# A block of four gated layers on one core: the second layer's projection in fp32, small inputs as rows, and a new order of the work

## The reference

```python
x = x + tanh(g_xattn[0]) * wkv(w, u, k=_layernorm(x), v=ctx_2048)          # a scan over 64 steps per sequence
x = x + tanh(g_ffn[0])   * ffn(_layernorm(x), w_gate_up, w_proj)
x = x + tanh(g_xattn[1]) * attention(_layernorm(x), ctx_2048, mask)
x = x + tanh(g_ffn[1])   * linear_fp8(_layernorm(x), weight, weight_scale, bias)

def ffn(x, w_gate_up, w_proj):             # hidden width 1024
    gate, up = split(x @ ternary_quant(w_gate_up).T)
    h = silu(gate) * up
    hn = h * rsqrt(mean(h * h) + eps)      # eps of float32
    return hn @ ternary_quant(w_proj).T
```

## Time and profile before

| | |
|---|---|
| median of the runs | 175.01 us |
| the profiled execution: device time, span from its first to its last instruction | 174.68 us, 172.9 us |
| busy of the span: PE, DVE, ACT, POOL | 120.4, 135.1, 72.5, 54.4 us |
| granted clock of TensorE, mean | 0.868 |
| chain that ended last, by engine | DVE 56%, PE 20%, issue 8%, DMA 6%, ACT 4%, POOL 2% |

### The profile page before, as it was taken

How to read it: one execution, slowest core, us unless ns; L and a number is a source line. 1 busy time by engine, 2 the same in 40 slices (tenths; PEclk the granted TensorE clock), 3 DMA queues, 4 the chain that set the end, 5 groups by cost and what they waited for, 6 DMA issues and landing times.

```text
span 172.9 us, 2109 instructions
## 1 busy us (share of the span) xinstructions
PE 120.4 (70%) x723; PEld 80.6 (47%) x729; DVE 135.1 (78%) x275; ACT 72.5 (42%) x122; POOL 54.4 (31%) x69
## 2 busy tenths in 40 slices
PE   6549980961069397298960999796988596894672
PEld 6447750840055152045630656363666385681451
DVE  0485997799959859999999947999968868933950
ACT  2333555485034438033360455663951125514322
POOL 5085033006000004130493519635442303400320
PEclk9987997598555879969997599999999969999698
DMA  3599910000000000000000000000000000000033
GB/s 93 146 365 353 327 39 2 0 0 0 0 0 0 0 0 4 0 0 2 0 0 4 2 0 0 0 2 4 0 0 0 0 4 0 0 2 0 0 121 125
DMA packets 8045, 6.90 MB, mean 40 GB/s; under 512 B 2273, under 2 KB 7778, under 8 KB 8034
## 3 DMA queue, kind: packets, MB, share of 16 engines
q1 hardware_dynamic: 7602, 6.75, 12.4%
q10 hardware_dynamic: 432, 0.00, 0.1%
HBM read 5.71 MB, written 1.05 MB: 39 GB/s over the span
## 4 chain that ended last, share of the span: by engine, by line
DVE 56%; PE 20%; issue 8%; DMA 6%; ACT 4%; POOL 2%; SPq 2%; DVEq 1%; ACTq 0%
DVE sums L1005 6%; DVE sums L1097 6%; DMA xs<-in_x_dram 6%; DVE stats L978 5%; DVE xn L990 5%; DVE xs L1025 5%; DVE hbuf L1091 4%; DVE wsign L1067 4%; PE ps L759 3%; PE ps L758 3%; DVE wmask L1066 3%; PE ps L779 3%; DVE wmask L1072 2%; DVE ratio L1010 2%; DVE kv L1322 2%
## 5 line engine op out<-in xcount | busy, mean ns | idle before, releaser
L758 PE MATMUL ps<-xhi,wT 128*128 128x512 f16 x64 | 25.9, 404 | 7.8 <-DVE wT L1056 4.4
L759 PE MATMUL ps<-xlo,wT 128*128 128x512 f16 x64 | 26.2, 410 | 0.0
L779 PE MATMUL ps<-wT,wgu_raw 128*128 128x256 bf16 x64 | 16.6, 298 | 6.1 <-DVE wT L1056 4.3
L536 ACT ACTIVATE wgu_raw<-hbuf 128x512 f16<-128x512 f32 x16 | 10.0, 627 | 24.7 <-DVE hbuf L1091 24.6
L978 DVE BATCH_NORM_STATS2 stats<-xs 128x6 f32<-128x256 f32 x32 | 12.2, 409 | 6.6 <-DMA xs<-in_x_dram 6.4
L1091 DVE SCALAR_TENSOR_TENSOR hbuf<-ps,pscale,sil 128x512 f32<-128x512 f32 x16 | 12.0, 749 | 6.3 <-PE ps L759 3.5
L779 PE MATMUL ps<-wT,sums 128*128 128x256 bf16 x64 | 16.6, 297 | 0.0
L412 POOL TENSOR_TENSOR sqsum<-sqsum,ratio 128x512 f32<-128x512 f32 x8 | 11.4, 1429 | 15.5 <-ACT ratio L539 15.2
L1097 DVE TENSOR_TENSOR sums<-hbuf,wgu_raw 128x512 f16<-128x512 f32 x16 | 15.8, 989 | 0.0
L531 ACT ACTIVATE sil<-ps 128x512 f32<-128x512 f32 x16 | 9.5, 592 | 12.5 <-PE ps L759 12.0
L758 PEld LDWEIGHTS ps<-xhi,wT 128*128 128x128 bf16 x64 | 6.5, 102 | 16.8 <-DVE wT L1056 4.9
(11 more groups left out here) (151 smaller groups left out, 281.5 us busy)
## 6 DMA issues: line engine op xcount, KB each, us to landing
wgu_raw<-in_L_ffn_w_gate_up_dram SPq DMA_DIRECT2D x4, 512.0 KB, 8.9
xs<-in_x_dram SPq DMA_DIRECT2D x2, 512.0 KB, 8.0
ctx_sb<-in_ctx_dram SPq DMA_DIRECT2D x2, 512.0 KB, 8.8
wp_raw<-in_L_ffn_w_proj_dram SPq DMA_DIRECT2D x1, 1024.0 KB, 10.1
out_dram<-xs SPq DMA_DIRECT2D x4, 256.0 KB, 2.2
wlin_raw<-in_L_ffn_weight_dram SPq DMA_DIRECT2D x1, 256.0 KB, 9.3
bias_bc<-in_L_ffn_bias_dram SPq DMA_DIRECT2D x1, 128.0 KB, 8.9
mask_u<-in_mask_BxS_bk_dram SPq DMA_DIRECT2D x2, 32.0 KB, 7.9
```

The source lines that it names most:

```text
L536: act.activation(hhi[:, h, j, :], hbuf[:, b, :], ACT.Copy).then_inc(hhi_ready, 1)
L758: pe.matmul(ps[:, 4 + 2 * b + up, :], w, xhi[:, h, c, :], start=(c == 0), stop=False)
L759: mm = pe.matmul(ps[:, 4 + 2 * b + up, :], w, xlo[:, h, c, :], start=False, stop=(c == CH - 1))
L779: mm = pe.matmul(ps[:, i // 2, o:o + C], part[:, h, j, i * P:(i + 1) * P], wp, start=(first and j == 0 and i % 2 == 0), stop=(not first an ...
```

## The change

- **Projection in fp32.** `ffn_mul` writes the product in fp32 into `hidden` (two tiles, one for each half) and multiplies by silu alone. `hhi`, `hlo`, `hbuf`, `ffn_low` and the ACT copy are gone; so is `pscale` with all that computes it. ACT makes an fp32 copy `wpf` of the two quantized pairs of w_proj (`project_weight`), and `project(h, j)` is 4 fp32 matmuls of 256 columns. Squares are taken from `hidden`.
- **Small inputs as rows.** Decay, bonus, gates, weight scale, mask and bias are loaded as one row each by ACT's queue, behind a table load. PE spreads them by matmuls of one row (`spread_rows`, `spread_mask`); POOL converts the mask row, ACT makes `mask_add` of it. The decay's matmul takes one fp32 row in place of three bf16 ones. x half 0 comes in two transfers.
- **A new order.** DVE runs `wkv(2)` before `mix_out(0)`, quantizes whole pairs in the order 0, 1, 4, 2, 3, 5 with the clip in front, takes `xn_low(0)` before `wkv(3)`, and leaves the normalization of the ffn input wholly to ACT. PE starts the projections earlier, and sends `spread_greatest` before the last `residual_back` and the warming matmuls. 32 warming transposes become 16 and 4; one group of 8 warming matmuls is gone.

```diff
 def ffn_mul(n):
-    if n >= 2:
-        dve.wait_ge(sq_ready, n - 1)
-        dve.wait_ge(hlo_ready, n - 1)
-    dve.scalar_tensor_tensor(out=hbuf[:, b, :], in0=ps[:, 5 + 2 * b, :], scalar=pscale[:, 0:1],
-                             in1=sil[:, b, :], op0=ALU.mult, op1=ALU.mult).then_inc(h_ready, 1)
-def ffn_low(n):
-    dve.tensor_tensor(hlo[:, h, j, :], hbuf[:, b, :], hhi[:, h, j, :], ALU.subtract).then_inc(hlo_ready, 1)
+    dve.tensor_tensor(hidden[n // HT][:, n % HT, :], ps[:, 5 + 2 * b, :], sil[:, b, :],
+                      ALU.mult).then_inc(h_ready, 1)
...
+def project_weight(a):          # ACT
+    act.wait_ge(wq_ready, QUANT_ORDER.index(GU_PAIRS + a) + 1)
+    act.activation(wpf[:, a, :], wT[:, GU_PAIRS + a, :], ACT.Copy).then_inc(wpf_ready, 1)
...
 def project(h, j):              # PE
-    pe.wait_ge(hlo_ready, h * HT + j + 1)
+    pe.wait_ge(wpf_ready, 1 + j // 4)
+    pe.wait_ge(h_ready, h * HT + j + 1)
     for i in range(TPC):
-        for part, first in ((hhi, True), (hlo, False)):
-            mm = pe.matmul(ps[:, i // 2, o:o + C], part[:, h, j, i * P:(i + 1) * P], wp, ...)
+        mm = pe.matmul(ps[:, i // 2, o:o + C], hidden[h][:, j, i * P:(i + 1) * P], wp, ...)
...
+def spread_rows():              # PE
+    pe.wait_ge(in_rows, 80)
+    for c in range(CH):
+        pe.matmul(wcol[:, c:c + 1], w_row[0:1, c * P:(c + 1) * P], ones_row[0:1, 0:1], ...)
+        pe.matmul(ucol[:, c:c + 1], u_row[0:1, c * P:(c + 1) * P], ones_row[0:1, 0:1], ...)
+    pe.matmul(ps[:, 1, 4:9], ones_row[0:1, :], g_row[0:1, 0:5], ...).then_inc(cols_ps, 1)
...
 # DVE's order from the second layer's quantization on
-weights_clip(4); weights_clip(5); gate_up_bound()
-wkv(3); quant_sign(0); quant_sign(1); xn_low(0); power_of_two()
+quant(0); quant(1); xn_low(0); wkv(3)
+dve.tensor_reduce(valid[:, :], mask_add[:, :, :], AX_X, ALU.max)
+quant(2)
...
 # PE's order
+gate_up(2); project(0, 0); gate_up(3); project(0, 1); y_back(1); project(0, 2)
+gate_up(4); project(0, 3); gate_up(5); gate_up(6)
 pe.wait_ge(res_ready[1], 2)
 channel_major(1, 2, TPC, TPC, 2, xnT_ps)
 project(0, 4)
+gate_up(7)
 project(0, 5); project(0, 6); gate_up(HT)
+project(0, 7)
 gate_up(HT + 1)
-project(0, 7)
...
 residual_back(2)
+spread_greatest()
 residual_back(3)
-pe.wait_ge(xn3T_ready, 2 * CH)
-keep_warm(WARM_LAST, 4, wT)
-spread_greatest()
+keep_warm(WARM_LAST, 5, wT)
```

More of the change, by code:

```diff
@@ L163, in gated_blocks @@
         res = xs
-        in_x = [sem("in_x0"), sem("in_x1")]
+        in_x = [sem(f"in_x{i}") for i in range(3)]
         in_ctx = [sem("in_ctx0"), sem("in_ctx1")]
@@ L273, in gated_blocks @@
         wlin_t = w_lin.rearrange("(o p) i -> p o i", p=P)
-        mask_t = mask.rearrange("(i two) m -> two i m", two=2)
+        mask_t = mask.rearrange("(a i two) m -> a i two m", a=1, two=2)
         ROW_GROUPS = [0, 2, 1, 3]
-        def act_scales(p):
-            return p + 1 if p == 0 else p
+        QUANT_ORDER = (0, 1, 4, 2, 3, 5)
         LAST_ORDER = (0, 1, 3, 2)
@@ L591, in _ @@
             softmax_exp(0)
+            square(CHUNKS * HT - 1)
             attn_in(0)
@@ L620, in _, with spread_mask @@
         def _(pe):
+            def spread_rows():
+                pe.wait_ge(const_ready, 1)
+                pe.wait_ge(in_rows, 80)
+                for c in range(CH):
+                    pe.matmul(wcol[:, c:c + 1], w_row[0:1, c * P:(c + 1) * P], ones_row[0:1, 0:1], start=True, stop=True)
+                    pe.matmul(ucol[:, c:c + 1], u_row[0:1, c * P:(c + 1) * P], ones_row[0:1, 0:1], start=True, stop=True)
+                pe.matmul(ps[:, 1, 4:9], ones_row[0:1, :], g_row[0:1, 0:5], start=True, stop=True).then_inc(cols_ps, 1)
+            def spread_mask():
+                pe.wait_ge(mask_row, 1)
+                for half in range(2):
+                    mm = pe.matmul(ps[64 * half:64 * half + 64, 7, :], ones_row_b[0:1, :], mb_row[0:1, :, half, :],
+                                   start=True, stop=True)
+                mm.then_inc(mask_ps_ready, 1)
             def front_values(h):
@@ L642, in front_keys @@
                                   start=(i == 0), stop=False, skip_group_check=True)
-                    for part in range(3):
-                        mm = pe.matmul(ps[:, c, :], ngparts[0:1, part, c * P:(c + 1) * P], t_row[0:1, :],
-                                       start=False, stop=(part == 2), skip_group_check=True)
-                    mm.then_inc(kT_ready, 1)
+                    pe.matmul(ps[:, c, :], ngrow[0:1, c * P:(c + 1) * P], t_row[0:1, :],
+                              start=False, stop=True, skip_group_check=True).then_inc(kT_ready, 1)
             def weight_transposes(p):
@@ L846, in _ @@
             pe.wait_ge(ident_ready, 1)
-            for _ in range(WARM_UP):
+            for _ in range(WARM_FIRST):
+                pe.transpose(ps[:, 7, 0:P], ident[:, :], ident[:, :])
+            spread_rows()
+            for _ in range(WARM_SECOND):
                 pe.transpose(ps[:, 7, 0:P], ident[:, :], ident[:, :])
@@ L904, in _ @@
             project(1, 2)
-            gate_up(HT + 6)
             channel_major(2, 1, *PARTS[0], qT_ps)
             project(1, 3)
+            gate_up(HT + 6)
+            project(1, 4)
+            scores(0)
             gate_up(HT + 7)
-            scores(0)
-            project(1, 4)
             project(1, 5)
```

371 lines of the change are left out of this document (143 added, 228 removed).

## The result

The changed kernel takes 162.86 us (median of 4 runs, 160.59 to 163.97) against 174.44 us for the kernel before on the same chip (4 runs, 173.4 to 180.55): a ratio of 0.927, with a 95% interval of 0.912 to 0.943. Forecast were 166.4 us, and 161 to 172. The ratios here leave disturbed runs out, the medians hold all runs, so the two need not divide exactly.

What follows compares the result with a forecast made beforehand. DVE was taken to bound stretches 1 and 2, PE stretch 3, and one chain of both stretch 4; -11.5 - 2.1 + 8.9 - 3.9 = -8.6 us gave 166.1 us profiled, 166.4 median, range 161 to 172.

Steps and rivals of the forecast that it cites:

- Stretch 1: Kernel start to the end of xn_low(0), where the first gate_up begins: DVE-bound, 58.8 to 47.3 us, 11.5 less.
- The start of the first wkv: On DVE in the front: from 18.17 to 15.2 us, 3.0 earlier; gain bounded between 1.4 and 3.5.
- The bound by the rows: Front: PE spreads rows after five ACT transfers land, the last at 11.2 us at worst, first wkv then near 16.8.
- Stretch 2: From the end of xn_low(0) to the fifth projection: DVE-bound, 36.4 to 34.3 us, 2.1 less.
- hits: DVE passes delayed by POOL passes in stretch 2: 0.95 us each, about four among twelve POOL passes, 3.5 us.
- Stretch 3: Fifth projection to the end of the last: PE-bound with fp32 passes, 33.9 to 42.8 us, 8.9 longer.
- two allowances: Added to PE's 39.3 us in stretch 3: 1.5 for half-clock time, 2.0 for waits on DVE's residual and normalization.
- The rival on the clock: Stretch 3: fp32 passes or waits keep PE at 1.2 GHz; for half the work 20 us more, 186 us; chance 0.07.
- that on exposed loads: Projections in stretch 3: 96 fp32 weight loads of 0.19 us not hidden, 18 us more, 184 us; chance 0.03.
- Stretch 4: The tail after the last projection: the spread moved ahead of residual_back(3) and warming shortens the chain by 3.9 us.
- 0.7 for the wait: Tail: the last maximum is taken from PSUM by DVE some 0.7 us after it was ready.
- more comes through: Rival: no stall in stretch 3 (3.5 us less) and half the hits (1.8 less), giving 161 us; chance 0.18.

Runs made afterwards that it cites:

- the repetition: The changed kernel run once more with nothing changed, as the measure for the other kernels of its call: 164.15 us (before on that chip 174.3).
- the columns kernel: The changed kernel also loading decay and bonus as columns of 4-byte values that nobody reads, on SP's queue: 163.56 us, ratio 0.937 to the kernel before.

## Why the prediction was right, and where it was not

**Stretch 1**, -11.5 forecast, -14.3 measured. The start of the first wkv was taken at 15.2. It is not one number: 12.9 to 13.1 us in the four executions in which the two groups of transposes ahead of it (context, then weights) took 1.1 us each, 13.9 to 16.0 in the eight in which one or both took 1.4 to 2.0. (The clock column can't be relied on there: in the repetition it shows 1.00 from 6 to 14 us, with both groups at 1.9.) PE's transposes and first keys stand in that path, and I had bounded only transfers and DVE's work. The bound by the rows did not bind: PE began to spread them between 4.9 and 6.8 us, where 11.2 was the worst. The profiled execution was one of the early ones; 2.3 of the 2.8 us are this. From the first wkv on the stretch became 9.0 us shorter, 8.55 forecast.

**Stretch 2**, 34.3 forecast, 33.04 measured. The five hits of DVE passes by POOL's (1.78, 1.64, 1.64 and twice 0.98 us, where 0.69 is the unhindered time, 0.75 for the last) make 3.5 us; 3.5 was forecast. The 1.3 us lie in DVE's own sum, where five products took 3.0 us and not 3.5, and four quantizations 15.6 and not 16.0. The product's 688 ns agrees with what the Trainium skill says of one SBUF input (SBUF — State Buffer, Who interferes with whom); that all twelve POOL passes would meet one did not happen (ten ran in the stretch).

**Stretch 3**, 42.8 forecast, 39.67 measured. The work was right: 39.3 forecast, 39.67 done. What failed are the two allowances, 1.5 for half clock and 2.0 for waits: PE never waited, since with 12 subtractions less DVE was busy 15.78 us and always ahead. The rival on the clock (0.07) and that on exposed loads (0.03) can be struck: clock 1.00, loads under the passes. The allowance for half clock was a chance and not an error, though: of the 11 profiled executions with the new order and fp32, eight took 39.67 or 39.68 us, and three 41.21, 41.36 and 42.73, with the fifth projection at half clock.

**Stretch 4**, -3.9 forecast, +0.7 measured: the step that failed, though not by its mechanism. At full clock the maximum is taken 1.07 us after it is ready (4.56 before), the old order costs 5.34, and the tail is 38.9 to 39.1 us, where it is at full clock to its end, and I had 39.9. I had 0.7 for the wait: the 0.3 to 0.4 on top come from the bias as a row, which I had put down as the same passes (with the matrix again it is 0.68). What I left out was the clock: I carried the tail's 0.91 of the earlier trace rows over as if it belonged to the work. It fell to 0.50 for ten microseconds instead of three, 3.8 us, and in the last matmuls cost 1.7 more.

The rival "more comes through" described the first three stretches better than my forecast did, by one of its two terms: there was no stall in stretch 3, but the hits were not halved. The tail's clock put the sum back near the forecast.

## What to carry to other kernels

An exchange of DVE passes for PE passes has no price of its own: here the same one gained 4.5 us in one order and lost 3.2 in another, so it has to be costed with the order that feeds PE. Read the granted clock stretch by stretch, also after a change that doesn't touch that stretch, and where idle gaps of PE stand ahead of a chain of its work, try filling them; 14 spare matmuls brought 4.4 us here by the medians, 1.7 of it in the last 24 matmuls. And cut stretches so that a moved step stays inside one: a gain that only crosses a cut is none.

## What the runs showed of the hardware

- A half clock, once there, lasted 10 us with PE busy 9.44 of them (131 to 141 us), and in the columns kernel over 15 us with PE busy 14.47 of 15.60 (126.4 to 142.0).
- Two fp32 matmuls of 256 columns with one row of weights take 1.05 us where those with 128 rows take 0.86, and the two of 128 rows behind them 0.97: fewer rows cost 0.3 us more a block, not less.
- fp32 weight loads of 205 ns lie wholly under passes of 0.215 us.
- 512 packets of 4 bytes more on SP's queue moved the first wkv by 0.2 us, which is also the spread of its early starts (12.90 to 13.12).
